# Band projections written out in eight trips, with turned rows copied straight to place and the norms regrouped

## Chip, cores and metric

One Trainium2 chip, one core. The metric is the device time of one launch in microseconds. Engines are named as the profile does: PE is TensorE, DVE VectorE, ACT ScalarE, POOL GpSimd, SP the queue that issues most DMAs.

## What is computed

The reference runs six residual blocks over x of shape (4, 1024, 128), float32. The fifth is a band attention; its beginning is what the changed function computes:

```python
invariant = _linear(x, Wproj, bproj)
residual = x - invariant
gauge = jnp.mean(jnp.linalg.norm(residual, axis=-1) / (jnp.linalg.norm(x, axis=-1) + 1e-08))
x_qk = jnp.where(gauge > GAUGE_THRESH, invariant, x)
Q = _linear(x_qk, Wq, bq)...
K = _linear(x_qk, Wk, bk)...
V = _linear(x, Wv, bv)...
```

Here x is the layer norm (without gain and bias) of the running rows: (x - m) / sqrt(v + 1e-5). The mean over all 4096 tokens must be known before the first Q and K row.

## The kernel before

The 4096 tokens lie in SBUF as X, 32 tiles of 128 tokens by 128 features. A trip takes 4 tiles (GROUP), so there are 8 trips; a block of 512 columns is the transposed rows of one trip. The stage runs from 1556.1 to 1636.7 us. Each engine has its own program, and counting semaphores alone set the order between them.

Before the first trip the outcome of the block in front is added to X: two partial results per token, in four quarters of 8 tiles (`add_back`, line 165), all on DVE. Quarter q holds the tiles of trips 2q and 2q + 1.

Trip j on each engine:
- DVE: `statistics(j)` (bn_stats, bn_aggr per tile) gives mean and variance; POOL turns variance into 1/sqrt (L2146, L2148, a power); DVE `normalise(j)` (L2167) writes xn.
- PE `turn_x(j)` (L2090) transposes four tiles into the PSUM bank x_ps. ACT `copy_x` (L2124) copies them to one of two buffers xs; DVE copies that buffer on to A.xnT (L2177).
- PE makes the gauge product inv_ps (L2096), 128x512; ACT adds the bias and stores it in A.invT (L2131); DVE forms res = x - invariant (L2182).
- ACT squares xs (L2129) and res (L2135); PE sums over features with a column of ones, eight matmuls of one column (L2108), each a weight load and a matmul in two passes, so 16 records a trip; DVE copies the eight columns from n_ps to A.norms (L2173).
- PE makes four value products v_ps (L2101); DVE adds the bias (L2186).

On PE the order in a trip is: gauge product of j, transposes of j+1, values of j, norms of j. The norms wait for both squares of j and, through `n_ready`, for DVE's copy of the norms of j-1, which stands behind the value copy of j on DVE. On ACT the order is: Square of xs (which waits for the norms of j-1), bias copy, copy_x of j+1, Square of res. Trips 1 to 4 are a hardware loop of two trips per pass, the others are written out. After the last trip ACT takes the square root of all norms, DVE adds 1e-8, inverts, multiplies and sums, PE adds up over partitions (L2116), and DVE compares with 0.3 into A.use_inv (L2222, L2224). The next stage, the queries (L2332 on), begins with that.

Of the kernel before, what the change touches and what calls it, by code (L numbers as in the profile page):

```python
# [12 lines left out]
ALU = mybir.AluOpType  # L13
# [3 lines left out]
P = 128  # L17
# [2024 lines left out]
def band_projections(nc, K, A, io, kept):  # L2042

    X, c = K.X, K.c
    with ExitStack() as ctx:
# [3 lines left out]
        stats, mv, var, rstd = sb("stats", [P, GROUP, 6]), sb("mv", [P, GROUP, 2]), sb("var", [P, GROUP]), sb("rstd", [P, GROUP])  # L2049
        xn, res = sb("xn", [P, GROUP, D]), sb("res", [P, BLOCK])  # L2050
        xs = [sb(f"xs{i}", [P, BLOCK]) for i in range(2)]
        squares = [sb(f"squares{m}", [P, BLOCK]) for m in range(2)]
        x_ps, inv_ps, v_ps, n_ps, w_ps, w_ps2 = (ps(n) for n in ("x_ps", "inv_ps", "v_ps", "n_ps", "w_ps", "w_ps2"))
        s = stage_sems(nc, ctx, "bp", "loaded passed turned kept ln_stats ln_mv ln_var ln_rstd xn_ready x_full xs_ready inv_full inv_ready "
                                     "v_full v_ready res_ready squares_ready n_full n_ready sqrt_ready gauge_step gauge_full joined")
        block = ctx.enter_context(nc.Block())
        SMALL = 10

        def in_projection_trips(eng, one_trip):

# [18 lines left out]
        @block.tensor  # L2079
        def _(pe):  # L2080
            for k in range(len(WEIGHTS)):
                bank = (w_ps, w_ps2)[k // 4]
                nc.tensor.transpose(bank[:, (k % 4) * P:(k % 4 + 1) * P], natural[:, k, :], c.ident[:, :])
            nc.tensor.transpose(w_ps2[:, P:P + 64], w1_natural[:, :], c.ident[0:64, 0:64]).then_inc(s.turned, 1)

            def turn_x(j):
                pe.wait_ge(s.xn_ready, j + 1)
                wait(pe, s.xs_ready, j)
                for t in range(GROUP):
                    last = nc.tensor.transpose(x_ps[:, t * P:(t + 1) * P], xn[:, t, :], c.ident[:, :])  # L2090
                last.then_inc(s.x_full, 1)

            def trip(j, p):
                pe.wait_ge(s.xs_ready, j + 1)
                wait(pe, s.inv_ready, j)
                nc.tensor.matmul(inv_ps[:, :], A.wT[:, 3, :], xs[p][:, :], start=True, stop=True).then_inc(s.inv_full, 1)  # L2096
                if not (isinstance(j, int) and j == TRIPS - 1):
                    turn_x(j + 1)
                wait(pe, s.v_ready, j)
                for t in range(GROUP):  # L2100
                    last = nc.tensor.matmul(v_ps[:, t * P:(t + 1) * P], xs[p][:, t * P:(t + 1) * P], A.wT[:, 2, :], start=(t == 0), stop=True,  # L2101
                                            skip_group_check=True)
                last.then_inc(s.v_full, 1)
                pe.wait_ge(s.squares_ready, at(j, 2, 2))
                wait(pe, s.n_ready, j)
                for t in range(GROUP):
                    for m in range(2):
                        last = nc.tensor.matmul(n_ps[:, 2 * t + m:2 * t + m + 1], squares[m][:, t * P:(t + 1) * P], A.ones[:, 0:1],  # L2108
                                                start=(t == 0 and m == 0), stop=True, skip_group_check=True)
                last.then_inc(s.n_full, 1)  # L2110

            turn_x(0)
            pe.wait_ge(s.kept, 3)
            in_projection_trips(pe, trip)
            pe.wait_ge(s.gauge_step, 5)
            nc.tensor.matmul(n_ps[:, 0:1], A.ones[:, :], A.norms[:, 0, 0:1], start=True, stop=True).then_inc(s.gauge_full, 1)  # L2116

        @block.scalar
        def _(act):
            def copy_x(j, p):  # L2120
                act.wait_ge(s.x_full, j + 1)
                wait(act, s.v_full, j - 1)
                wait(act, s.res_ready, j - 1)
                nc.scalar.copy(xs[p][:, :], x_ps[:, :]).then_inc(s.xs_ready, 1)  # L2124

            def trip(j, p):
                act.wait_ge(s.xs_ready, j + 1)
                wait(act, s.n_full, j)
                nc.scalar.activation(squares[1][:, :], xs[p][:, :], ACT.Square).then_inc(s.squares_ready, 1)  # L2129
                act.wait_ge(s.inv_full, j + 1)  # L2130
                nc.scalar.activation(A.invT[:, bass.ds(j * BLOCK, BLOCK)], inv_ps[:, :], ACT.Identity, bias=proj_bias).then_inc(s.inv_ready, 1)  # L2131
                if not (isinstance(j, int) and j == TRIPS - 1):
                    copy_x(j + 1, 1 - p)
                act.wait_ge(s.res_ready, j + 1)
                nc.scalar.activation(squares[0][:, :], res[:, :], ACT.Square).then_inc(s.squares_ready, 1)  # L2135

            copy_x(0, 0)
            in_projection_trips(act, trip)
            act.wait_ge(s.n_ready, TRIPS)
            nc.scalar.activation(A.norms[:, :, :], A.norms[:, :, :], ACT.Sqrt).then_inc(s.sqrt_ready, 1)  # L2140

        @block.gpsimd
        def _(pool):
            def trip(j, p):
                pool.wait_ge(s.ln_mv, j + 1)
                nc.gpsimd.tensor_tensor(var[:, :], mv[:, :, 1], c.eps[:, 0:GROUP], ALU.add).then_inc(s.ln_var, 1)  # L2146
                pool.wait_ge(s.ln_var, j + 1)
                nc.gpsimd.tensor_tensor(rstd[:, :], var[:, :], c.minus_half[:, 0:GROUP], ALU.pow).then_inc(s.ln_rstd, 1)  # L2148

            in_trips(pool, trip)  # L2150

        @block.vector
        def _(dve):
            def statistics(j):
                for t in range(GROUP):
                    last = nc.vector.bn_stats(stats[:, t, :], X[:, j * GROUP + t, :])
                last.then_inc(s.ln_stats, 1)
                wait_alone(dve, s.ln_stats, j + 1, s.passed)
                for t in range(GROUP):
                    last = nc.vector.bn_aggr(mv[:, t, :], stats[:, t, :])  # L2160
                last.then_inc(s.ln_mv, 1)

            def normalise(j):
                dve.wait_ge(s.ln_rstd, j + 1)
                wait(dve, s.x_full, j)
                for t in range(GROUP):
                    last = nc.vector.tensor_scalar(xn[:, t, :], X[:, j * GROUP + t, :], mv[:, t, 0:1], rstd[:, t:t + 1],  # L2167
                                                   ALU.subtract, ALU.mult)
                last.then_inc(s.xn_ready, 1)

            def keep_norms(j):
                dve.wait_ge(s.n_full, j + 1)
                nc.vector.tensor_copy(A.norms[:, bass.ds(j * GROUP, GROUP), :], n_ps[:, 0:2 * GROUP].rearrange("p (t m) -> p t m", m=2)).then_inc(s.n_ready, 1)  # L2173

            def trip(j, p):
                dve.wait_ge(s.xs_ready, j + 1)
                nc.vector.tensor_copy(A.xnT[:, bass.ds(j * BLOCK, BLOCK)], xs[p][:, :])  # L2177
                if not (isinstance(j, int) and j == TRIPS - 1):
                    normalise(j + 1)
                dve.wait_ge(s.inv_ready, j + 1)  # L2180
                wait(dve, s.squares_ready, at(j, 2, 0))
                nc.vector.tensor_tensor(res[:, :], xs[p][:, :], A.invT[:, bass.ds(j * BLOCK, BLOCK)], ALU.subtract).then_inc(s.res_ready, 1)  # L2182
                if not (isinstance(j, int) and j >= TRIPS - 2):
                    statistics(j + 2)
                dve.wait_ge(s.v_full, j + 1)
                nc.vector.tensor_tensor(A.v[:, bass.ds(j * GROUP + 1, GROUP), :], v_ps[:, :].rearrange("p (t d) -> p t d", d=P),  # L2186
                                        v_bias.unsqueeze(1).broadcast_to([P, GROUP, P]), ALU.add).then_inc(s.v_ready, 1)
                if not (isinstance(j, int) and j == 0):
                    keep_norms(j - 1)

            nc.vector.memset(A.ones[:, :], 1.0)
            nc.vector.memset(A.tiny[:, :], 1e-10)
# [5 lines left out]
            statistics(0)  # L2198
            normalise(0)
# [839 lines left out]
```

## Time and profile before

| | |
|---|---|
| median of 3 runs | 2554.82 us (2554.65 to 2556.2) |
| profiled execution, first to last instruction | 2555.3 us |
| mean granted TensorE clock | 0.838 |
| busy share PE / DVE / ACT / POOL | 78% / 77% / 55% / 41% |
| the stage | 80.6 us, 3.2% of the span |

The profile is one execution, recorded in hardware. Its span lies 0.5 us above the median of the runs. The shares are averages over stages with different limits and say little about this one; here the timeline of single engines counts.
### The profile page before, as it was taken

The numbers are of one execution on the slowest core, as the hardware profiler recorded it, in microseconds if no ns is written. First come the engines' busy times: TensorE is split into PE (matmuls) and PEld (weight loads), VectorE is DVE, ScalarE is ACT, GpSimd is POOL, SyncE is SP. The second block draws the span as 40 slices with busy tenths as digits, with TensorE's granted clock in tenths as the row PEclk, the third lists the DMA queues.
The fourth block names the chain that finished last, engine by engine and source line by source line (L and its number), as shares of the span: only waits on it lengthen the run. The fifth ranks groups of instructions, "written<-read, shape, count | busy, mean of one in ns | idle before, by whom it ended". The sixth has DMA issues, their size and how long they took to land. (4 is left out here: it accounts for less than half of the span.)

```text
span 2555.3 us, 85621 instructions
## 1 busy us (share of the span) xinstructions
PE 2005.7 (78%) x34294; PEld 1619.8 (63%) x34294; DVE 1955.3 (77%) x4641; ACT 1416.9 (55%) x2304; POOL 1039.6 (41%) x961
## 2 busy tenths in 40 slices
PE   3779399999999998669578994764666667769994
PEld 3668388888888887558457993552222234547894
DVE  5889589999999997779764444597999978855443
ACT  1647244444444443447455551367999978737452
POOL 3757355544444453666565662004000000036563
PEclk7889699999999998679879996685555578869997
DMA  5133200000000000022332222003333200031324
GB/s 124 47 98 111 86 3 0 0 0 0 0 0 0 0 0 3 31 82 88 117 105 81 70 69 81 0 0 52 63 50 63 35 2 1 2 90 46 92 77 122
DMA packets 103658, 120.90 MB, mean 47 GB/s; under 512 B 23224, under 2 KB 85288, under 8 KB 102848
## 3 DMA queue, kind: packets, MB, share of 16 engines
q1 hardware_dynamic: 82544, 80.39, 13.1%
q0 software_dynamic: 18176, 37.79, 4.4%
q8 instruction: 96, 1.57, 0.2%
q10 hardware_dynamic: 2768, 0.55, 0.2%
q14 instruction: 74, 0.61, 0.1%
HBM read 60.00 MB, written 46.20 MB: 42 GB/s over the span
## 5 line engine op out<-in xcount | busy, mean ns | idle before, releaser
L2521 DVE CUSTOM_DVE_ANT_0 be_logs<-be_joint,be_logs 128x1024 f32<-128x1024 f32 x256 | 293.3, 1222 | 10.2 <-ACT be_logs L2504 9.2
L2504 ACT ACTIVATE be_logs<-be_joint,b_tiny 128x1024 f32<-128x1024 f32 x256 | 283.7, 1114 | 19.7 <-PE be_joint L2489 11.8
L2489 PE MATMUL be_joint<-be_parts_k,be_parts_q 64*128 64x512 f32 x512 | 202.3, 789 | 108.9 <-DVE be_sums L2521 91.4
L446 POOL DMA_INDIRECT d_pairs<-s_y_tile,s_x_tiles x156 | 178.7, 1145 | 128.9 <-DVE s_y_tile L1404 104.4
L2489 PEld LDWEIGHTS be_joint<-be_parts_k,be_parts_q 64*128 64x128 f32 x512 | 73.7, 285 | 237.3 <-DVE be_sums L2521 216.5
L1764 POOL TENSOR_TENSOR m_roped_q<-m_raw_q,kg_xn 128x512 f32<-128x512 f32 x64 | 82.4, 1288 | 327.0 <-ACT m_raw_q L1686 327.0
L559 POOL IOTA s_xn<- 128x32 int32 x2 | 0.5, 253 | 487.1 <-POOLq L63 487.1
L446 POOL DMA_INDIRECT d_pairs<-g_y_tile,g_x_tiles x156 | 158.0, 1013 | 92.4 <-ACT g_y_tile L894 60.9
L1404 DVE TENSOR_SCALAR s_y_tile<-s_ps_y,s_x_tiles 128x128 f32<-128x128 f32 x156 | 47.5, 346 | 149.1 <-PE s_ps_y L1238 149.1
L1238 PE MATMUL s_ps_y<-s_down,s_a_tile 128*128 x1248 | 151.7, 275 | 0.0
L1238 PEld LDWEIGHTS s_ps_y<-s_down,s_a_tile 128*128 128x128 f32 x1248 | 145.9, 192 | 0.0
L1515 PE MATMUL m_front<-m_xnT,m_w_rot 128*128 128x128 f32 x1024 | 143.4, 284 | 3.2 <-DVE m_turned_q L1820 3.2
L1314 ACT ACTIVATE s_a_tile<-s_ps_h,s_tile_bias 128x256 f32<-128x256 f32 x312 | 122.5, 475 | 34.9 <-PE s_ps_h L1221 34.9
L1515 PE MATMUL m_front<-m_xnT,kg_xn 128*128 128x128 f32 x1024 | 138.9, 284 | 0.6 <-ACT m_xnT L1671 0.6
L1515 PEld LDWEIGHTS m_front<-m_xnT,m_w_rot 128*128 128x128 f32 x1024 | 126.0, 194 | 7.6 <-DVE m_turned_q L1820 3.4
L1515 PEld LDWEIGHTS m_front<-m_xnT,kg_xn 128*128 128x128 f32 x1024 | 124.1, 195 | 6.8 <-DVE m_w_rot L1955 0.9
L1724 ACT COPY m_oT<-m_back 128x1024 f32<-128x1024 f32 x32 | 32.5, 1017 | 127.1 <-PE m_back L1614 127.1
L1686 ACT COPY m_raw_q<-m_front 128x512 f32<-128x512 f32 x64 | 37.5, 585 | 111.1 <-PE m_front L1515 111.1
L776 PE MATMUL g_ps_h<-g_x_hi,g_up_tile 128*128 128x256 f32 x312 | 97.4, 312 | 1.5 <-DVE g_up_tile L1012 0.5
L1219 PE MATMUL s_ps_h<-s_x_hi,s_up_tile 128*128 128x256 f32 x312 | 96.0, 308 | 3.1 <-issue 3.1
L1909 DVE TENSOR_TENSOR m_mem<-m_mem,m_back 128x1040 f32<-128x1040 f32 x64 | 78.7, 1230 | 15.0 <-PE m_back L1598 14.6
L1220 PE MATMUL s_ps_h<-s_x_hi,s_up_tile 128*128 128x256 f32 x312 | 89.3, 286 | 0.0
(501 smaller groups left out, 6303.7 us busy)
## 6 DMA issues: line engine op xcount, KB each, us to landing
g_x_tiles<-d_rows SPq DMA_DIRECT2D x78, 132.0 KB, 2.1
s_x_tiles<-d_rows SPq DMA_DIRECT2D x78, 132.0 KB, 2.1
d_rows<-d_rows SPq DMA_DIRECT2D x32, 132.0 KB
s_down<-L_ffn_We SPq DMA_DIRECT2D x16, 256.0 KB, 6.0
be_parts_q<-be_high_q SPq DMA_DIRECT2D x64, 64.0 KB, 2.3
be_parts_q<-b_soft_q SPq DMA_DIRECT2D x64, 64.0 KB, 2.3
be_parts_k<-be_high_k SPq DMA_DIRECT2D x60, 64.0 KB, 2.3
be_parts_k<-b_soft_k SPq DMA_DIRECT2D x60, 64.0 KB, 2.3
```

The lines of the kernel that those rows point to most:

```text
L446: nc.gpsimd.indirect_dma_start(out=pairs[:, :], out_offset=bass.IndirectOffsetOnAxis(ap=x_tile[i % LOADS_AHEAD][:, h, D:D + 1].bitcast(U32 ...
L776: nc.tensor.matmul(h, up_tile[b][:, 0, m, part, :], x_hi[b][:, 0:SLOT_ROWS], start=(k % 2 == 0), stop=False, skip_group_check=True)
L1219: nc.tensor.matmul(h, up_tile[b][:, 0, chunk], x_hi[b][:, 0:SLOT_ROWS], start=(k % 2 == 0), stop=False, skip_group_check=True)
L1220: nc.tensor.matmul(h, up_tile[b][:, 1, chunk], x_hi[b][:, 0:SLOT_ROWS], start=False, stop=False, skip_group_check=True)
L1238: last = nc.tensor.matmul(y, a_tile[b][:, k, h * P:(h + 1) * P], down[:, bass.ds(experts[i], 1), k * D:(k + 1) * D], start=False, stop=(k ...
L1314: nc.scalar.activation(a_tile[b][:, k, :], ps_h[2 * b + k // 2][:, (k % 2) * SLOT_ROWS:(k % 2 + 1) * SLOT_ROWS], ACT.Silu, bias=tile_bias[ ...
L1515: last = nc.tensor.matmul(front_ps[bank][:, k * P:(k + 1) * P], weights[:, column + k * P:column + (k + 1) * P], xnT[:, :], start=(k == 0) ...
L1764: nc.gpsimd.tensor_tensor(roped[k][:, part, :], raw[k][:, part, :], wide(cos).broadcast_to([P, 4, P]), ALU.mult).then_inc(s.cos_done, 1)
L1909: nc.vector.tensor_tensor(part, part, back_ps[:, :, 0:4 * AUG].rearrange("p b (c e) -> p b c e", e=AUG), ALU.add).then_inc(s.mem_done, 1)
L2489: last = nc.tensor.matmul(joint_ps[k % DEPTH][:, a, :], parts[b % 2][0][rows, i * P:(i + 1) * P], parts[b % 2][1][rows, half * 512:(half + ...
L2504: nc.scalar.activation(logs[k % DEPTH][:, :, :], joint_ps[k % DEPTH][:, :, :], ACT.Ln, bias=A.tiny[:, :]).then_inc(s.log_ready, 1)
L2521: nc.vector.tensor_tensor_reduce(out=flat, in0=joint_ps[k % DEPTH][:, :, :].rearrange("p a j -> p (a j)"), in1=flat, scale=1.0, scalar=0.0 ...
```

## The change

1. The transposed rows are copied from PSUM straight into A.xnT, whose block j then serves as operand; the buffers xs and the copy L2177 go.
2. The residual norms of trip j are summed on PE behind the values of trip j+1, into columns of n_ps of their own for all 32 tiles; the copies to A.norms in each trip go, and the root reads PSUM.
3. The norm of x is taken from the layer norm: 128 times variance times 1/(v + 1e-5). The Square of x and half of the norm matmuls go; two small DVE operations come in trip 6.
4. The statistics have room for all 32 tiles, and all eight trips are written out on every engine.
5. The additions of quarters 2 and 3 move from DVE to POOL (`add_late`), four of 128x1024. DVE does statistics(1) ahead of normalise(0).
6. A first root on one column stands at the start of ACT's program; the x norms' root and reciprocal need not wait for the last residual norms.

```diff
+        xs = [A.xnT[:, j * BLOCK:(j + 1) * BLOCK] for j in range(TRIPS)]
+        inv = [A.invT[:, j * BLOCK:(j + 1) * BLOCK] for j in range(TRIPS)]
...
+            def residual_norms(j):
+                pe.wait_ge(s.squares_ready, j + 1)
                 for t in range(GROUP):
-                    for m in range(2):
-                        last = nc.tensor.matmul(n_ps[:, 2 * t + m:2 * t + m + 1], squares[m][:, t * P:(t + 1) * P], A.ones[:, 0:1],
+                    last = nc.tensor.matmul(n_ps[:, j * GROUP + t:j * GROUP + t + 1], squares[:, t * P:(t + 1) * P], A.ones[:, 0:1],
...
+            for j in range(TRIPS):
+                gauge_input(j)
+                if j + 1 < TRIPS:
+                    turn_x(j + 1)
+                values(j)
+                if j:
+                    residual_norms(j - 1)
+            residual_norms(TRIPS - 1)
...
+            act.wait_ge(s.warmed, 1)
+            nc.scalar.activation(warm[:, :], A.tiny[:, :], ACT.Sqrt)
+            copy_x(0)
+            for j in range(TRIPS):
+                act.wait_ge(s.inv_full, j + 1)
+                nc.scalar.activation(inv[j], inv_ps[:, :], ACT.Identity, bias=proj_bias).then_inc(s.inv_ready, 1)
+                if j + 1 < TRIPS:
+                    copy_x(j + 1)
+                act.wait_ge(s.res_ready, j + 1)
                 wait(act, s.n_full, j)
+                nc.scalar.activation(squares[:, :], res[:, :], ACT.Square).then_inc(s.squares_ready, 1)
+            act.wait_ge(s.norm_step, 2)
+            nc.scalar.activation(A.norms[:, :, 1], x_norm[:, :], ACT.Sqrt).then_inc(s.sqrt_ready, 1)
+            act.wait_ge(s.n_full, TRIPS)
+            nc.scalar.activation(A.norms[:, :, 0], n_ps[:, 0:TILES], ACT.Sqrt).then_inc(s.sqrt_ready, 1)
...
+            def add_late(q):
+                pool.wait_ge(kept.back_in[q], 32)
+                for m in range(2):
+                    if m:
+                        pool.wait_ge(s.joined_late, 2 * (q - 2) + 1)
+                    nc.gpsimd.tensor_tensor(X[:, quarter(q), :], X[:, quarter(q), :], kept.back[m][:, quarter(q), :], ALU.add).then_inc(s.joined_late, 1)
+
+            inverse_deviations(0)
+            inverse_deviations(1)
+            add_late(2)
+            inverse_deviations(2)
+            add_late(3)
+            for j in range(3, TRIPS):
+                inverse_deviations(j)
...
-            for q in range(1, 4):
-                add_back(nc, dve, X, kept.back, q, kept.back_in[q], s.joined)
-            dve.wait_ge(s.joined, 8)
-            statistics(1)
-            in_projection_trips(dve, trip)
-            keep_norms(TRIPS - 1)
+            add_back(nc, dve, X, kept.back, 1, kept.back_in[1], s.joined)
+            dve.wait_ge(s.joined, 4)
+            for j in range(TRIPS):
+                if j + 1 < TRIPS:
+                    normalise(j + 1)
+                residual(j)
+                if j + 2 < TRIPS:
+                    statistics(j + 2)
...
+                keep_values(j)
```

On TensorE before, trips 1 and 2 in the loop body (bp_inv_ps is the gauge product, bp_x_ps the transposes, bp_v_ps the values, bp_n_ps the norms):

```order
L2096 MATMUL bp_inv_ps<-bp_xs,b_wT 128x512
L2087 REGISTER_ALU
L2090 MATMUL bp_x_ps<-ident,bp_xn 128x128 x4
L2101 MATMUL bp_v_ps<-b_wT,bp_xs 128x128 x4
L2104 ISA
L2108 MATMUL bp_n_ps<-b_ones,bp_squares 128x1 x8
L2096 MATMUL bp_inv_ps<-bp_xs,b_wT 128x512
```

And in the changed kernel, trips 0 and 1:

```order
L2091 MATMUL bp_inv_ps<-b_xnT,b_wT 128x512
L2085 MATMUL bp_x_ps<-ident,bp_xn 128x128 x4
L2096 MATMUL bp_v_ps<-b_wT,b_xnT 128x128 x4
L2091 MATMUL bp_inv_ps<-b_xnT,b_wT 128x512
L2085 MATMUL bp_x_ps<-ident,bp_xn 128x128 x4
L2096 MATMUL bp_v_ps<-b_wT,b_xnT 128x128 x4
L2103 MATMUL bp_n_ps<-b_ones,bp_squares 128x1 x4
```

The norms have moved behind the values of the next trip, and there are four matmuls of them, not eight.

On GpSimd, the start of its program in the stage, as a difference (bp_rstd is 1/sqrt of a trip; ks_wide and ks_xn are the two partial results added to X):

```order
 L2146 TENSOR_TENSOR bp_var<-bp_mv,eps 128x4
 L2148 TENSOR_TENSOR bp_rstd<-bp_var,minus_half 128x4
-L2145 REGISTER_ALU
+L2155 TENSOR_TENSOR X<-X,ks_wide 128x1024
+L2155 TENSOR_TENSOR X<-X,ks_xn 128x1024
 L2146 TENSOR_TENSOR bp_var<-bp_mv,eps 128x4
 L2148 TENSOR_TENSOR bp_rstd<-bp_var,minus_half 128x4
-L73 REGISTER_ALU
-L73 COMPARE_AND_BRANCH
+L2155 TENSOR_TENSOR X<-X,ks_wide 128x1024
+L2155 TENSOR_TENSOR X<-X,ks_xn 128x1024
```

Two additions stand between the second and the third 1/sqrt, two more between the third and the fourth.

## Rows read from the trace of the kernel before

**Rows 1.** Busy time by stretch: the trips 1 to 7, then the query stage.

```profile
core 0: us, PE busy (x) PEld busy (x) DVE busy (x) ACT busy (x) POOL busy (x), PEclk, DMA share, GB/s
...
1580.10:1633.10 53.00, 43.09 (x207) 35.02 (x206) 23.43 (x90) 18.31 (x28) 6.03 (x10) 0.71 0.00 0
...
1636.70:1722.00 85.30, 55.81 (x221) 43.37 (x222) 78.89 (x100) 48.95 (x61) 0.00 (x0) 0.80 0.00 0
```

**Rows 2.** Timeline of PE: start, duration, line, tiles, idle before and releaser.

```profile
1576.37 1.92 PE L2101 MATMUL bp_v_ps<-b_wT,bp_xs 128*128 128x128 f32 x8
...
1580.04 1.10 PE L2096 MATMUL bp_inv_ps<-bp_xs,b_wT 128*128 128x512 f32 x2
1580.98 0.60 PE L2090 MATMUL bp_x_ps<-ident,bp_xn 128*128 128x128 f32 x4
1581.42 1.06 PE L2101 MATMUL bp_v_ps<-b_wT,bp_xs 128*128 128x128 f32 x8
1584.99 3.14 PE L2108 MATMUL bp_n_ps<-b_ones,bp_squares 128*128 128x1 f32 x16 [2.52 <-DVE b_norms L2173]
1587.99 2.05 PE L2096 MATMUL bp_inv_ps<-bp_xs,b_wT 128*128 128x512 f32 x2
...
1616.40 3.55 PE L2108 MATMUL bp_n_ps<-b_ones,bp_squares 128*128 128x1 f32 x16 [1.01 <-DVE b_norms L2173]
1619.81 2.05 PE L2096 MATMUL bp_inv_ps<-bp_xs,b_wT 128*128 128x512 f32 x2
...
1626.65 2.06 PE L2096 MATMUL bp_inv_ps<-bp_xs,b_wT 128*128 128x512 f32 x2
...
1631.13 1.92 PE L2108 MATMUL bp_n_ps<-b_ones,bp_squares 128*128 128x1 f32 x16 [0.95 <-DVE b_norms L2173]
```

**Rows 3.** Waits in the stage: who for whom, us in total, times, longest.

```profile
PE bp_n_ps L2108 <- DVE b_norms L2173: 9.9, 7, 2.5
```

**Rows 4.** Timeline of ACT in trip 2.

```profile
1590.18 0.69 ACT L2131 ACTIVATE b_invT<-bp_inv_ps,ks_xn 128x512 f32 x1 [1.32 <-PE bp_inv_ps L2096]
1590.94 0.58 ACT L2124 COPY bp_xs<-bp_x_ps 128x512 f32<-128x512 f32 x1
1591.81 0.63 ACT L2135 ACTIVATE bp_squares<-bp_res 128x512 f32<-128x512 f32 x1 [0.29 <-DVE bp_res L2182]
```

**Rows 5.** Timeline of DVE: an addition and normalise(1) at the start, then trip 3.

```profile
1564.10 1.22 DVE L165 TENSOR_TENSOR X<-X,ks_wide 128x1024 f32<-128x1024 f32 x1
...
1574.29 1.11 DVE L2167 TENSOR_SCALAR bp_xn<-X,bp_mv,bp_rstd 128x128 f32<-128x128 f32 x4 [1.18 <-POOL bp_rstd L2148]
...
1598.75 0.69 DVE L2182 TENSOR_TENSOR bp_res<-bp_xs,b_invT 128x512 f32<-128x512 f32 x1 [3.02 <-ACT b_invT L2131]
1599.36 0.87 DVE L2156 BATCH_NORM_STATS2 bp_stats<-X 128x6 f32 x4
...
1602.15 1.11 DVE L2167 TENSOR_SCALAR bp_xn<-X,bp_mv,bp_rstd 128x128 f32 x4 [0.42 <-POOL bp_rstd L2148]
```

**Rows 6.** Groups of POOL by form: busy, mean ns of one, idle before.

```profile
L1769 POOL TENSOR_TENSOR m_roped_q<-m_roped_q,m_turned_q 128x1024 f32<-128x1024 f32 x32 | 75.8, 2369 | 0.0
...
L2148 POOL TENSOR_TENSOR bp_rstd<-bp_var,minus_half 128x4 f32<-128x4 f32 x8 | 8.1, 1011 | 0.6
```

**Rows 7.** Timeline of POOL and DVE in the memory stage, where both work.

```profile
287.40 1.62 POOL L1764 TENSOR_TENSOR m_roped_q<-m_raw_q,kg_xn 128x512 f32<-128x512 f32 x1 [1.02 <-ACT m_raw_q L1686]
...
287.97 1.07 DVE L1963 TENSOR_SCALAR m_one_less_beta<-m_beta 128x16 f32<-128x16 f32 x1
...
305.86 3.46 POOL L1769 TENSOR_TENSOR m_roped_k<-m_roped_k,m_turned_k 128x512 f32<-128x512 f32 x2 [4.22 <-DVE m_turned_k L1820]
...
308.13 2.28 DVE L165 TENSOR_TENSOR X<-X,kg_wide 128x1024 f32<-128x1024 f32 x1
```

**Rows 8.** Timeline of DVE behind the last norms.

```profile
1633.09 0.17 DVE L2173 COPY b_norms<-bp_n_ps 128x8 f32<-128x8 f32 x1 [2.10 <-PE bp_n_ps L2108]
...
1634.62 0.15 DVE L2220 COPY b_norms<-b_gate 128x1 f32<-128x1 f32 x1
...
1635.65 0.15 DVE L2224 TENSOR_SCALAR b_use_inv<-b_use_inv 128x1 f32<-128x1 f32 x1
```

More of the change, by code:

```diff
@@ L2091, in turn_x, with gauge_input, values @@
                 last.then_inc(s.x_full, 1)
-            def trip(j, p):
+            def gauge_input(j):
                 pe.wait_ge(s.xs_ready, j + 1)
                 wait(pe, s.inv_ready, j)
-                nc.tensor.matmul(inv_ps[:, :], A.wT[:, 3, :], xs[p][:, :], start=True, stop=True).then_inc(s.inv_full, 1)
-                if not (isinstance(j, int) and j == TRIPS - 1):
-                    turn_x(j + 1)
+                nc.tensor.matmul(inv_ps[:, :], A.wT[:, 3, :], xs[j], start=True, stop=True).then_inc(s.inv_full, 1)
+            def values(j):
                 wait(pe, s.v_ready, j)
                 for t in range(GROUP):
-                    last = nc.tensor.matmul(v_ps[:, t * P:(t + 1) * P], xs[p][:, t * P:(t + 1) * P], A.wT[:, 2, :], start=(t == 0), stop=True,
+                    last = nc.tensor.matmul(v_ps[:, t * P:(t + 1) * P], xs[j][:, t * P:(t + 1) * P], A.wT[:, 2, :], start=(t == 0), stop=True,
                                             skip_group_check=True)
                 last.then_inc(s.v_full, 1)
-                pe.wait_ge(s.squares_ready, at(j, 2, 2))
-                wait(pe, s.n_ready, j)
+            def residual_norms(j):
+                pe.wait_ge(s.squares_ready, j + 1)
                 for t in range(GROUP):
-                    for m in range(2):
-                        last = nc.tensor.matmul(n_ps[:, 2 * t + m:2 * t + m + 1], squares[m][:, t * P:(t + 1) * P], A.ones[:, 0:1],
-                                                start=(t == 0 and m == 0), stop=True, skip_group_check=True)
+                    last = nc.tensor.matmul(n_ps[:, j * GROUP + t:j * GROUP + t + 1], squares[:, t * P:(t + 1) * P], A.ones[:, 0:1],
+                                            start=(j == 0 and t == 0), stop=True, skip_group_check=True)
                 last.then_inc(s.n_full, 1)
@@ L2118, in _, with copy_x @@
+            pe.wait_ge(s.gauge_step, 4)
+            nc.tensor.matmul(n_ps[:, 2 * TILES:2 * TILES + 1], A.ones[:, :], A.gate[:, :], start=True, stop=True, skip_group_check=True).then_inc(s.gauge_full, 1)
         @block.scalar
         def _(act):
-            def copy_x(j, p):
+            def copy_x(j):
                 act.wait_ge(s.x_full, j + 1)
-                wait(act, s.v_full, j - 1)
-                wait(act, s.res_ready, j - 1)
-                nc.scalar.copy(xs[p][:, :], x_ps[:, :]).then_inc(s.xs_ready, 1)
@@ L2126, in trip @@
-            def trip(j, p):
-                act.wait_ge(s.xs_ready, j + 1)
-                wait(act, s.n_full, j)
[L2129 to L2140, printed above, removed]
+                nc.scalar.copy(xs[j], x_ps[:, :]).then_inc(s.xs_ready, 1)
+            act.wait_ge(s.warmed, 1)
[7 more added lines that the diff above has]
+                act.wait_ge(s.res_ready, j + 1)
+                wait(act, s.n_full, j)
+                nc.scalar.activation(squares[:, :], res[:, :], ACT.Square).then_inc(s.squares_ready, 1)
@@ L2154, in statistics @@
             def statistics(j):
-                for t in range(GROUP):
-                    last = nc.vector.bn_stats(stats[:, t, :], X[:, j * GROUP + t, :])
+                if j in (4, 6):
+                    dve.wait_ge(s.joined_late, j - 2)
+                for t in range(j * GROUP, (j + 1) * GROUP):
+                    last = nc.vector.bn_stats(stats[:, t, :], X[:, t, :])
                 last.then_inc(s.ln_stats, 1)
                 wait_alone(dve, s.ln_stats, j + 1, s.passed)
-                for t in range(GROUP):
+                for t in range(j * GROUP, (j + 1) * GROUP):
                     last = nc.vector.bn_aggr(mv[:, t, :], stats[:, t, :])
@@ L2166, in normalise @@
                 for t in range(GROUP):
[L2167 to L2168 removed]
+                    w = j * GROUP + t
+                    last = nc.vector.tensor_scalar(xn[:, t, :], X[:, w, :], mv[:, w, 0:1], rstd[:, w:w + 1], ALU.subtract, ALU.mult)
                 last.then_inc(s.xn_ready, 1)
[L2171 to L2173 removed]
@@ L2175, in trip, with keep_values @@
[L2175 to L2179, printed above, removed]
-                dve.wait_ge(s.inv_ready, j + 1)
[L2181 to L2189, printed above, removed]
+            def keep_values(j):
+                dve.wait_ge(s.v_full, j + 1)
+                nc.vector.tensor_tensor(A.v[:, j * GROUP + 1:(j + 1) * GROUP + 1, :], v_ps[:, :].rearrange("p (t d) -> p t d", d=P),
+                                        v_bias.unsqueeze(1).broadcast_to([P, GROUP, P]), ALU.add).then_inc(s.v_ready, 1)
@@ L2191, in _, with residual @@
+            def residual(j):
+                dve.wait_ge(s.inv_ready, j + 1)
+                wait(dve, s.squares_ready, j)
+                nc.vector.tensor_tensor(res[:, :], xs[j], inv[j], ALU.subtract).then_inc(s.res_ready, 1)
+            nc.vector.memset(A.tiny[:, :], 1e-10).then_inc(s.warmed, 1)
             nc.vector.memset(A.ones[:, :], 1.0)
-            nc.vector.memset(A.tiny[:, :], 1e-10)
             for padded in (A.v, A.knT):
@@ L2198, in _ @@
             statistics(0)
+            statistics(1)
             normalise(0)
```

40 lines of the change are left out of this document (18 added, 22 removed).

## The prediction

> **What bounds the stage now.** I read the engines' totals by stretch first, because the change lies in one stage of some 80 us out of 2555.3: 1556.1 to 1636.7 us. From the first full trip to the last norm the stretch takes 53.0 us; TensorE is busy 43.1 of it, VectorE 23.4, ScalarE 18.3, at a mean granted clock of 0.71 [rows 1]. I call the start of trip j's gauge product on TensorE T(j). The timeline of TensorE gives T(1) = 1580.04, T(2) = 1587.99, T(6) = 1619.81, T(7) = 1626.65 [rows 2], so a trip lasts 8.0 us on the mean and the last full one 6.8. The reader is to see the gap before the norm products: in trip 1 TensorE waits 2.52 us there, and the grouped waits put 9.9 us in seven such gaps on the copy of the last trip's norms [rows 2, 3]. Behind the norm products stand the next gauge product and, on ScalarE, the squares of x and the copy of the next rows. So one trip is one ring: gauge product, ScalarE's bias copy, VectorE's residual, statistics, value copy and norm copy, sixteen norm records, next gauge product. TensorE cannot be kept full because the norms of trip j stand ahead of the gauge product of trip j+1.
>
> **Prices of TensorE's parts.** The two clock levels both stand in the rows (1.2 GHz is granted 0.5, 2.4 GHz is 1.0). The length of an operation, measured to the next start, is about 0.2 us less than the duration shown. At the low level: gauge product 1.85 (2.05 shown), value products 1.7 (1.92 shown), norms 3.41 (1616.40 to 1619.81). At the high level: 0.94, transposes 0.44, values 0.86, norms 1.77 (1.92 shown, less 0.15) [rows 2]. Transposes at the low level are twice 0.44, about 0.88.
>
> **Part by part.**
> Norms of x from the statistics: eight of the sixteen norm records of a trip go, so 1.7 us at the low clock and 0.88 at the high one; a Square of 0.63 us leaves ScalarE, which is not full. Norms a trip later: the wait of 9.9 us in all goes. Rows copied to place: 0.42 us of VectorE a trip, and the norm copy of 0.15 goes too; VectorE has the room already.
>
> *The new ring.* TensorE's own work in a trip is at the low clock 1.85 + 0.88 + 1.7 + 1.7 = 6.1 us, at the high clock 0.94 + 0.44 + 0.86 + 0.88 = 3.1. What is late next is the statistics chain, which spans two trips: gauge product (1.1 high, 2.05 low), ScalarE's bias copy with handoff 0.83, residual with handoff 0.74 [rows 4, 5], from the statistics' start to the start of normalise 2.79 (1599.36 to 1602.15, with GpSimd's power between), normalise 1.15, then transposes, values, norms 2.2 (high) up to T(j+2). That is 8.8 us per two trips, 4.4 a trip, at the high clock; at the low one 2.05 + 0.83 + 0.74 + 2.79 + 1.15 + 4.3 = 11.9, 5.9 a trip, so there TensorE's 6.1 binds. VectorE needs 1.1 + 0.6 + 1.3 + 0.6 = 3.6 a trip and does not bind. Which level? Full stretches of the old loop had 0.71 with TensorE busy 81%; the query stage after it has 0.80 with TensorE busy only 65% [rows 1]. The new ring at the high level is busy 3.1 of 4.4, 71%, with gaps of about 1.3 us instead of 2.5. I take about 0.85, that is 70% of the time high, and 4.9 us a trip. Bounds: 4.4 and 6.1.
>
> *The start, where I expect a cost.* Until T(0) nothing changes; statistics(1) goes into a wait of VectorE for GpSimd. Then VectorE adds back only quarter 1 instead of quarters 1 to 3: four additions of 1.22 us and 0.03 between, about 5 us, leave it, and normalise(1), at 1574.29 before [rows 5], could start at 1566.6. But the four additions run on GpSimd now, where a 128x1024 addition took 2.37 us [rows 6]; the first starts at about 1563.6, 1.5 us after statistics(1), by when GpSimd has its second power of 1.01 us [rows 6] behind it. The trace of the memory stage shows what happens when both engines read SBUF: GpSimd's product ran 287.40 to 289.02, and a VectorE tensor_scalar of only 128x16 begun at 287.97 took 1.07 us, to the same end; VectorE's addition of this very line, 1.22 us alone, took 2.28 us beside GpSimd's pair at 305.86 to 309.32 [rows 7]. They take turns. So I let them alternate: GpSimd 63.6 to 65.95, VectorE's first addition to 67.05, GpSimd's second to 69.3, VectorE's second to 70.4 (instead of 66.5). Normalise(1) to 71.5, residual(0) to 72.1, statistics(2) to 73.5, GpSimd's power to 74.8. There GpSimd goes on with the third addition, to 77.3, ahead of normalise(2), which VectorE reaches at 75.1 (values of trip 0 done) and which reads X: one of its four parts gets in at 77.3, the rest behind the fourth addition, 80.6. Transposes 0.9, values 1.7, norms of trip 0 1.7 at the low clock: T(2) = 1584.9. Against 1587.99 that is 3.1 us. If the two engines did not meet at all, the same chain gives T(2) = 1576.5. These are the ends; if every part of normalise(2) waited and handoffs grew, 1586.
> The Trainium skill (SBUF — State Buffer, "SBUF: two separate sides") holds that GpSimd and VectorE share a port pair as an exclusive lock for the whole instruction, and counts both a two-input VectorE operation and a two-port mode of tensor_scalar among the losers. That rule speaks against moving additions to GpSimd, and the memory stage agrees (1.07 us for 128x16). By it the start costs the 8.4 us between the two T(2); without it nothing.
>
> *Trips 2 to 6.* T(2) to T(7) took 1626.65 - 1587.99 = 38.7 us; now 5 x 4.9 = 24.5. Gain 14.2 (bounds 8.2 and 16.7).
>
> *The last trip.* From T(7) to the last norm record it was 6.4 us (1631.13 + 1.92 - 1626.65) [rows 2]. Now values, norms of trip 6 and, behind the last Square, norms of trip 7: 4.5 at the high clock, 6.9 at the low one; I take 5.3. Gain 1.1.
>
> *The tail.* From the last norm record at 1633.05 to the end of the second use_inv at 1635.80 it was 2.75 us [rows 8]. The copy out of PSUM (0.17 and 0.04), the addition (0.18), the reciprocal (0.35 + 0.04) and the copy of the sum (0.15) leave the path, since the x norms are ready early; root, product, sum, matmul, compare stay: 0.29 + 0.23 + 0.22 + 0.64 + 0.39 = 1.77. Gain 1.0. The table load of the root moves to the stage's start, where ScalarE is idle until 1564.5; it was hidden before too: nothing. The two small VectorE operations of x_norm in trip 6 lie in VectorE's gap before the values: nothing, 0.4 us without that cover.
>
> Sum: 3.1 + 14.2 + 1.1 + 1.0 = 19.4 us of the profiled 2555.3 us. The median of the runs, 2554.82, lies 0.5 below that span; I take the gain off the median: 2535.4 us.
>
> **Rivals.**
> *The additions don't collide.* For it: GpSimd's short power operations never lengthened a VectorE copy in this stage. Against it: rows 7. T(2) = 1576.5, 8.4 us more gain: 2527.
> *TensorE stays at the low level.* For it: the trips at 0.5 in the old loop followed directly on stretches in which TensorE had been held up, and trip 2 begins so. Against: 65% busy sufficed for 0.80 in the next stage. 5 x 6.1 = 30.5, last trip 6.9: 7.6 us less gain: 2543.
> *Written-out code gains by itself.* The old trips show no price of the loop: T(1) to T(2), inside the body, took 7.95; the four trips T(2) to T(6), two of them over the branch back, averaged 7.96 [rows 2]. So it gives nothing in my sum. If branches had held up engines other than TensorE, 4.4 a trip would be reached: 2532. The Trainium skill (Runtime: NRT & Kernel Launch, "Instruction fetch mechanics") says that a taken branch breaks sequential prefetch and calls this one reason for unrolling; by that rule the written-out form is the faster, which the two averages do not bear out.
> *The ring only moves its wait.* If residual, squares and bias copy on ScalarE in their new order hold each other up, trips stay above 7 us: 5 x 7.4 = 37, gain 1.7 instead of 14.2, and with the waits at the start not above 3: about 2551. Against it: ScalarE has 1.9 us of work a trip.
> *Slower: the query stage.* It lasts 85.3 us, VectorE is busy 78.9 of it and TensorE 55.8 at 0.80 [rows 1]. If its clock stayed at 0.5 after the changed entry, TensorE's work would be 55.8 x 0.8 / 0.5 = 89 us, more than the stage, and with the waits of one for the other about 110: 25 us more, 6 more than the change gives: 2560. It decides from a mean clock in that stage below about 0.55. Against it: nothing in that stage is touched, and it starts at 0.5 now.
>
> **Chances.** Forecast 0.58 (own range 2531 to 2540), no collision 0.16, low clock 0.16, code gain 0.04, wait moved 0.04, slower 0.02. 0.2%, 5.1 us, is about what this measurement can tell from no change. Faster 0.94, same 0.04, slower 0.02. The range 2525 to 2543.5 leaves out the last two and the ends of the second and third.
>
> **What would show it.** Right: GpSimd rows of 128x1024 at about 1563.6 and 1575, VectorE's quarter-1 additions with about 1.9 and 3.3 us, T(2) near 1585, then trips of 4.4 to 6 us with no wait before the norm products, transposes waiting on normalise instead; a tail of 1.8 us. Wrong: additions of 1.22 us beside GpSimd's; a clock of 0.5 from T(2) to T(7); trips above 7; or a query stage that differs from 85.3 us by more than 2.

## The result, and the profile after

| | before | changed |
|---|---|---|
| median | 2554.74 us (2554.15 to 2556.2, 4 runs) | 2530.57 us (2527.92 to 2534.04, 4 runs) |
| ratio, 95% interval | | 0.9905 [0.989, 0.992] |
| span of the profiled execution | 2555.3 us | 2526.1 us |
| the stage, first weight transpose to first query operation | 80.5 us | 57.7 us |

The change gains 24.2 us by the medians; forecast were 19.4, to 2535.4 us. The stage itself gains 22.9 us in the profiled executions. The spans differ by 29.2 us, and the other 6.3 lie in stages whose code is the same: the stage begins 2.1 us earlier, from its end to the first entropy product it is 113.1 instead of 114.4 us, and from the last entropy product to the end 508.5 instead of 511.3. These pieces wander: the kernel of experiment 4, whose last stages are those of before, had 507.1 where before had 511.3. So I judge by the stage from here on.

With j's start T(j) counted from the first weight transpose, the four terms of the sum came out so:

| | before | forecast | changed |
|---|---|---|---|
| to T(2) | 31.8 us | 28.8 | 27.2 |
| T(2) to T(7) | 38.7 | 24.5 | 23.3 |
| T(7) to the last norm record | 6.4 | 5.3 | 4.6 |
| tail to the second use_inv | 2.75 | 1.77 | 1.58 |

Busy time by stretch in the changed kernel, trips 1 to 7 and the query stage (answering to rows 1; the columns are the same):

```profile
1571.80:1609.23 37.43, 28.41 (x159) 22.39 (x158) 26.61 (x83) 12.63 (x21) 11.29 (x13) 0.84 0.00 1
1611.71:1697.00 85.29, 58.01 (x227) 45.80 (x228) 78.88 (x100) 49.06 (x61) 0.00 (x0) 0.78 0.00 0
```

TensorE's busy time fell from 43.1 to 28.4 us, and the stretch by 15.6 us: its waits are hardly shorter in sum, 9.0 against 9.9 us. The granted clock is 0.84 instead of 0.71 [rows 1]. The second stretch is cut to the length of that of before, so its length says nothing; its clock is 0.78 instead of 0.80, and the query stage up to the first entropy product took 113.1 instead of 114.4 us.

Timeline of PE, trips 2 to 6 of the changed kernel (answering to rows 2):

```profile
1581.28 1.10 PE L2091 MATMUL bp_inv_ps<-b_xnT,b_wT 128*128 128x512 f32 x2
...
1584.62 1.10 PE L2091 MATMUL bp_inv_ps<-b_xnT,b_wT 128*128 128x512 f32 x2
1587.71 1.11 PE L2085 MATMUL bp_x_ps<-ident,bp_xn 128*128 128x128 f32 x4 [2.00 <-DVE bp_xn L2183]
1588.62 1.91 PE L2096 MATMUL bp_v_ps<-b_wT,b_xnT 128*128 128x128 f32 x8
1590.33 1.17 PE L2103 MATMUL bp_n_ps<-b_ones,bp_squares 128*128 128x1 f32 x8
1591.36 1.10 PE L2091 MATMUL bp_inv_ps<-b_xnT,b_wT 128*128 128x512 f32 x2
...
1594.54 1.10 PE L2091 MATMUL bp_inv_ps<-b_xnT,b_wT 128*128 128x512 f32 x2
1597.79 1.12 PE L2085 MATMUL bp_x_ps<-ident,bp_xn 128*128 128x128 f32 x4 [2.15 <-DVE bp_xn L2183]
```

There is no wait before the norms of trips 0 to 6 any more; only the last group waits, 0.78 us for its Square. The wait stands before the transposes, on normalise, in every second trip: trips 2 to 6 last 3.34, 6.74, 3.18, 6.98 and 3.10 us. The short ones were granted 1.00, the long ones 0.75 and 0.76. Two trips together are 10.1 us, the two-trip chain of statistics at a mixed clock (8.8 and 11.9 were its ends). In the grouped waits of the stage, five waits for normalise, those of the start among them, stand where rows 3 had seven for the copy of the norms:

```profile
PE bp_x_ps L2085 <- DVE bp_xn L2183: 17.8, 5, 5.6
...
PE bp_n_ps L2103 <- ACT bp_squares L2136: 0.8, 1, 0.8
```

The start, first DVE and then POOL (answering to rows 5 to 7):

```profile
1562.02 2.67 DVE L165 TENSOR_TENSOR X<-X,ks_wide 128x1024 f32<-128x1024 f32 x1
1564.72 3.25 DVE L165 TENSOR_TENSOR X<-X,ks_xn 128x1024 f32<-128x1024 f32 x1
1568.01 1.12 DVE L2183 TENSOR_SCALAR bp_xn<-X,bp_mv,bp_rstd 128x128 f32<-128x128 f32 x4
...
1572.65 5.07 DVE L2183 TENSOR_SCALAR bp_xn<-X,bp_mv,bp_rstd 128x128 f32<-128x128 f32 x4
```

```profile
1561.26 2.35 POOL L2155 TENSOR_TENSOR X<-X,ks_wide 128x1024 f32<-128x1024 f32 x1
1563.69 3.20 POOL L2155 TENSOR_TENSOR X<-X,ks_xn 128x1024 f32<-128x1024 f32 x1
...
1572.38 2.34 POOL L2155 TENSOR_TENSOR X<-X,ks_wide 128x1024 f32<-128x1024 f32 x1
1574.80 2.34 POOL L2155 TENSOR_TENSOR X<-X,ks_xn 128x1024 f32<-128x1024 f32 x1
```

The turns can be read off the ends of the rows. GpSimd's first addition ends at 1563.61, VectorE's, begun at 1562.02, at 1564.69: 1.08 us after it. GpSimd's second begins at 1563.69, waits for that and ends at 1566.89; VectorE's second ends 1.08 us after that again. Normalise(2), four small operations of 0.34 us each, takes 5.07 us until both of GpSimd's other additions are through. Its first operation ends between the two additions, and the second lasts 2.49 us.

The tail on DVE (answering to rows 8):

```profile
1608.29 0.18 DVE L2226 TENSOR_SCALAR b_norms<-b_norms 128x32 f32<-128x32 f32 x1 [0.51 <-ACT b_norms L2138]
...
1609.58 0.19 DVE L2231 TENSOR_TENSOR b_curv<-b_curv,b_norms 128x32 f32<-128x32 f32 x1 [0.72 <-ACT b_norms L2140]
...
1610.66 0.15 DVE L2237 TENSOR_SCALAR b_use_inv<-b_use_inv 128x1 f32<-128x1 f32 x1
```

The addition and the reciprocal for the x norms run while the last residual norms are still being made, and 1.58 us are left behind 1609.23, where these end.

### The profile page after: what moved, and what is told of

It is laid out like the page before. It is cut to its first block and busy times, and to the rows that moved or that the text cites. A ratio compares the mean times of both kernels' runs of the same rounds, so it can differ in the third digit from the quotient of the medians.

```text
span 2526.1 us, 85364 instructions
## 1 busy us (share of the span) xinstructions
PE 1983.1 (79%) x34230; PEld 1601.6 (63%) x34230; DVE 1953.4 (77%) x4622; ACT 1412.7 (56%) x2298; POOL 1056.9 (42%) x965
## 5 line engine op out<-in xcount | busy, mean ns | idle before, releaser
L1724 ACT COPY m_oT<-m_back 128x1024 f32<-128x1024 f32 x32 | 32.6, 1018 | 127.0 <-PE m_back L1614 127.0
L1219 PE MATMUL s_ps_h<-s_x_hi,s_up_tile 128*128 128x256 f32 x312 | 95.9, 308 | 3.2 <-issue 1.6
L1769 POOL TENSOR_TENSOR m_roped_k<-m_roped_k,m_turned_k 128x512 f32<-128x512 f32 x64 | 88.3, 1392 | 6.2 <-DVE m_turned_k L1820 5.2
```

The costliest lines, as they stand in the source:

```text
L1219: nc.tensor.matmul(h, up_tile[b][:, 0, chunk], x_hi[b][:, 0:SLOT_ROWS], start=(k % 2 == 0), stop=False, skip_group_check=True)
L1769: nc.gpsimd.tensor_tensor(roped[k][:, part, :], roped[k][:, part, :], turned[k][:, part, :], ALU.add).then_inc(s.rope_done, 1)
```

## The experiments

Stage times are from one profile each. The time ratios are to the kernel before, on the same chip. All runs are in this table; the last two ran on a chip on which the kernel before took 2648.7 us. The experiments ran on three chips and there is one profile of the kernel before, so stage times of different chips stand side by side. The changed kernel's stage, profiled on two chips, was 57.7 and 58.2 us.

| | stage us | to T(2) | T(2) to T(7) | clock there | ratio, 95% interval |
|---|---|---|---|---|---|
| before | 80.5 | 31.8 | 38.7 | 0.68 | |
| changed | 57.7 | 27.2 | 23.3 | 0.85 | 0.9905 [0.989, 0.992] |
| 1 additions on DVE, in pairs | 57.9 | 18.6 | 32.2 | 0.73 | 0.9922 [0.9903, 0.9941] |
| 2 no late additions | 50.4 | 18.6 | 24.7 | 0.86 | 0.9868 [0.9852, 0.9885] |
| 3 norms in the same trip | 58.8 | 27.9 | 23.9 | 0.90 | 0.9917 [0.9901, 0.9934] |
| 4 before, written out | 83.7 | 32.6 | 40.6 | 0.62 | 0.9997 [0.9981, 1.0012] |
| 5 x squares back | 66.7 | 29.6 | 25.8 | 0.87 | 0.9929 [0.9909, 0.995] |
| 6 statistics ahead | 56.3 | 27.7 | 21.2 | 0.88 | 0.9881 [0.9851, 0.9911] |
| 7 statistics ahead, pairs on DVE | 54.8 | 18.0 | 29.7 | 0.77 | 0.988 [0.9849, 0.9911] |
| 8 before, own columns | 68.0 | 31.4 | 27.7 | 0.82 | 0.9939 [0.9919, 0.9959] |
| 9 one addition a trip | 50.5 | 18.9 | 24.3 | 0.86 | 0.9887 [0.9859, 0.9916] |
| 10 changed, again | 58.2 | 27.9 | 22.8 | 0.93 | 0.9925 [0.9899, 0.9951] |

**1. The additions on VectorE.**

```diff
-            add_late(2)
-            add_late(3)
...
                 if j in (4, 6):
-                    dve.wait_ge(s.joined_late, j - 2)
+                    add_back(nc, dve, X, kept.back, j // 2, kept.back_in[j // 2], s.joined)
+                    dve.wait_ge(s.joined, j + 2)
```

> Changed kernel, but the additions of quarters 2 and 3 stay on VectorE, each ahead of the statistics that need it (trips 2 and 4). Theory (exclusive turns of GpSimd and VectorE at SBUF): VectorE's quarter-1 additions fall from 2.67 and 3.25 us to 1.2 each, normalise(2) from 5.07 to 1.1 us, T(2) comes 6 to 7 us earlier; the two pairs of additions (2.5 us each) then lie in the statistics chain of trips 2 and 4 and cost 2 to 5 us; the stage lasts 53 to 56 us instead of 57.7. Rival (GpSimd's help is worth its price, VectorE binds): stage 58 to 62 us.

DVE in that kernel:

```profile
1565.04 1.21 DVE L165 TENSOR_TENSOR X<-X,ks_wide 128x1024 f32<-128x1024 f32 x1
1566.29 1.23 DVE L165 TENSOR_TENSOR X<-X,ks_xn 128x1024 f32<-128x1024 f32 x1
...
1572.34 1.12 DVE L2182 TENSOR_SCALAR bp_xn<-X,bp_mv,bp_rstd 128x128 f32<-128x128 f32 x4
...
1578.77 1.22 DVE L165 TENSOR_TENSOR X<-X,ks_wide 128x1024 f32<-128x1024 f32 x1
1580.03 1.23 DVE L165 TENSOR_TENSOR X<-X,ks_xn 128x1024 f32<-128x1024 f32 x1
...
1584.08 1.11 DVE L2182 TENSOR_SCALAR bp_xn<-X,bp_mv,bp_rstd 128x128 f32<-128x128 f32 x4 [0.82 <-POOL bp_rstd L2148]
```

The collision is shown: without GpSimd's additions VectorE's take 1.2 us, normalise(2) 1.12 instead of 5.07, and T(2) comes 8.6 us earlier (expected were 6 to 7; the forecast's ends lay 8.4 apart). But the expected stage of 53 to 56 us missed: T(2) to T(7) takes 8.9 us more, not 2 to 5. Trips 3 and 5, each behind a pair, last 8.9 and 8.7 us; TensorE waits 3.6 and 3.9 us in them, and the clock from T(2) to T(7) is 0.73. The pair stands between X and the statistics of a later trip and lengthens the chain itself. As ordered, GpSimd's help was worth what it cost, 57.7 against 57.9 us.

**2. Without those additions** (both `add_late` calls and the waits for them left out; that part of the sum is missing).

> Changed kernel without the additions of quarters 2 and 3 (that part of the computation is left out). It prices them by themselves. Theory: GpSimd's additions cost only through the turns, 3.9 us in the quarter-1 additions and 3.9 in normalise(2), less a wait of TensorE: stage 57.7 - 7 = about 51 us. Rival (additions beside each other cost no more than VectorE's own work): stage within 1 us of 57.7.

50.4 us, as expected: the four additions cost the changed kernel 7.3 us. T(2) comes 8.6 us earlier without them, and 1.3 of that are lost again from T(2) to T(7).

**3. Norms in the same trip.**

```diff
                 values(j)
-                if j:
-                    residual_norms(j - 1)
-            residual_norms(TRIPS - 1)
+                residual_norms(j)
```

> Changed kernel with the residual norms of trip j again behind the values of trip j. Theory (the statistics chain over two trips binds now, not the norms): the short trips grow from 3.2 to about 4.3 us and the long ones shrink by as much, stage within 1.5 us of 57.7. Rival (the norms a trip later are the main gain): each trip from T(2) on gains the wait of square and residual, 1 us or more, stage 62 us or longer.

1.2 us longer, within the 1.5 expected and no more than one profile can tell. Norms wait again (2.5 us in five trips), but in time in which the next normalise is not done anyway. No worth of the norms a trip later by themselves is shown here.

**4. Before, written out** (`for j in range(TRIPS): one_trip(j, j % 2)` in place of the loop, on all engines).

> Kernel before with all eight trips of the stage written out and nothing else changed. Theory (the loop costs nothing): stage within 1 us of 80.6, time within 2 us of the kernel before. Rival (taken branches break prefetch, computed addresses cost): stage 3 us or more shorter.

The time ratio is 0.9997, so writing out gives nothing that the interval of 5 us less to 3 us more can tell. The stage was 3.2 us longer, against the expectation of 1 us, in the same order of work: some trips had norms of 3.5 us at 0.5 where before had 1.9 at 1.0, though the waits before the norms were shorter, 8.1 against 9.9 us. A stage's length is known to some 3 us only, as its clock falls.

**5. The x squares back.** The Square stands behind that of the residual, its four sums in front of the residual's.

```diff
+                nc.scalar.activation(squares_x[:, :], xs[j], ACT.Square).then_inc(s.squares_x_ready, 1)
...
+                pe.wait_ge(s.squares_x_ready, j + 1)
+                for t in range(GROUP):
+                    nc.tensor.matmul(n_ps[:, TILES + j * GROUP + t:TILES + j * GROUP + t + 1], squares_x[:, t * P:(t + 1) * P], A.ones[:, 0:1],
```

> Changed kernel with the Square of x on ScalarE and its four sums a trip on TensorE done again, beside the norm from the statistics (their result is not used). Theory (TensorE's norm records lie on the two-trip chain: transposes, values, norms): 0.9 us a record group at the high clock, 1.7 at the low one, in every second trip, and twice at the end: stage 4 to 8 us longer than 57.7. Rival (norms are hidden in TensorE's waits): under 2 us.

9.0 us longer, just above the 4 to 8 expected: 2.4 before T(2), 2.4 up to T(7), and 4.0 in the last trip, which has 8.6 us: both groups of records and the second Square stand at its end one behind the other. So the half of the norm work that the change saves would not have been hidden.

**6. Statistics ahead.**

```diff
-                residual(j)
                 if j + 2 < TRIPS:
                     statistics(j + 2)
-                else:
+                residual(j)
+                if j + 2 >= TRIPS:
```

> Changed kernel with statistics(j+2) ahead of residual(j) on VectorE, nothing else. Theory (from T(2) on the chain bias copy, residual, statistics, power, normalise binds): without its first links the long trips of 6.7 to 7.0 us shrink; all trips 3.4 to 4.0 us, T(2) to T(7) 17 to 20 us instead of 23.3, stage 52 to 55 us. Rival (VectorE's amount of work or TensorE's clock binds): within 1.5 us of 57.7.

DVE and then POOL in that kernel, trips 4 and 5:

```profile
1594.39 0.66 DVE L2194 TENSOR_TENSOR bp_res<-b_xnT,b_invT 128x512 f32<-128x512 f32 x1
...
1596.23 1.11 DVE L2183 TENSOR_SCALAR bp_xn<-X,bp_mv,bp_rstd 128x128 f32<-128x128 f32 x4 [0.58 <-POOL bp_rstd L2148]
```

```profile
1594.55 0.55 POOL L2146 TENSOR_TENSOR bp_var<-bp_mv,eps 128x4 f32<-128x4 f32 x1 [2.53 <-DVE bp_mv L2175]
```

After a trip of 5.51 us at 0.55 and one of 3.11 at 1.00, three trips last 4.18, 4.18 and 4.17 us at 1.00, and T(2) to T(7) is 21.2 us. The expectation missed: it had trips of 3.4 to 4.0 us, T(2) to T(7) in 17 to 20 and a stage of 52 to 55, and 56.3 lies where the rival had it, 1.4 us below the changed kernel, which one profile does not tell from no change. Even trips alone prove nothing either, as the changed kernel has them in experiment 10. What differs is their length at the same clock, 4.18 against 4.42 us, and the gap before the transposes, 0.87 against 1.11.

The rows show what binds now: normalise waits 0.58 us for the power of its own statistics, and from normalise to normalise VectorE and GpSimd take 4.17 us without TensorE. Part of it is a new collision: GpSimd's short addition in front of the power (L2146) stands beside the residual and takes 0.55 us instead of 0.20. Without that the round would be 3.8 us by this estimate, inside the expected range; no run tests it.

**7. Both** (the edits of experiments 1 and 6).

> Statistics ahead and the additions of quarters 2 and 3 on VectorE together. Theory: the start is 8 us shorter as with the additions on VectorE alone; with the statistics ahead each pair of additions delays the ring by its own 2.5 us at most and not by a chain of 3.9 and a slower clock: stage 48 to 51 us, faster than both kernels. Rival (VectorE is then full): 53 us or more.

54.8 us, above the expected 48 to 51 and in the rival's range: trips 3 and 5, each the one behind a pair, last 8.0 and 8.7 us. The pair still stood ahead of the statistics in the same trip.

**8. Before, written out, with columns of their own.**

```diff
-                wait(pe, s.n_ready, j)
...
-                        last = nc.tensor.matmul(n_ps[:, 2 * t + m:2 * t + m + 1], squares[m][:, t * P:(t + 1) * P], A.ones[:, 0:1],
-                                                start=(t == 0 and m == 0), stop=True, skip_group_check=True)
+                        last = nc.tensor.matmul(n_ps[:, at_column:at_column + 1], squares[m][:, t * P:(t + 1) * P], A.ones[:, 0:1],
+                                                start=(j == 0 and t == 0 and m == 0), stop=True, skip_group_check=True)
```

Here `at_column` is `2 * (j * GROUP + t) + m`; the copies by `keep_norms` go.

> Kernel before, written out, with columns of their own for all 32 tiles' norms in PSUM, so that TensorE no longer waits for VectorE's copy of the last norms; 16 norm records a trip and all else as before. Theory (that wait, 9.9 us in seven trips, was the largest single loss): stage 74 to 78 us where the written-out kernel had 83.7. Rival (the squares come no sooner, the wait only changes its name): 82 us or more.

PE in that kernel, trips 2 and 5:

```profile
1592.38 1.10 PE L2092 MATMUL bp_inv_ps<-bp_xs,b_wT 128*128 128x512 f32 x2
...
1595.65 1.95 PE L2104 MATMUL bp_n_ps<-b_ones,bp_squares 128*128 128x1 f32 x16 [0.56 <-ACT bp_squares L2131]
...
1612.55 1.95 PE L2104 MATMUL bp_n_ps<-b_ones,bp_squares 128*128 128x1 f32 x16 [0.84 <-ACT bp_squares L2131]
```

68.0 us, 15.7 less than the written-out kernel and 12.6 less than before, with nothing else of the order changed: more than the 74 to 78 us expected. The waits before the norms had been 9.9 us in before and 8.1 in experiment 4; 2.7 are left, for squares. So the waits alone do not make the gain. From T(2) to T(7) TensorE's idle time falls from 6.4 us (6.2 in experiment 4) to 1.7, and its busy time, with the same records, from 32.3 (34.4) to 26.0. The larger part of the gain there, 6.3 to 8.4 us against 4.5 to 4.7, is the clock, 0.82 instead of 0.68 and 0.62. In experiment 8 the norms from trip 1 on take 1.93 to 2.17 us, in 4 up to 3.54.

**9. One addition a trip.** As 7, but without `add_back` in `statistics`; instead:

```diff
                 residual(j)
+                if j < 4:
+                    add_one(2 + j // 2, j % 2)
```

where `add_one(q, m)` is one of the two additions of quarter q.

> Statistics ahead, and the four additions of quarters 2 and 3 on VectorE one by one, behind the residuals of trips 0 to 3, where VectorE waits for the values or for GpSimd's power. Theory: no addition lies between X and the statistics of the next trips any more; each adds 0.6 us to a trip of 4.2 to 4.5 and no jump to 8 us as with pairs; T(2) at 18.5 to 19.5, T(2) to T(7) 21 to 24, stage 50 to 52 us. Rival (VectorE's 3.6 us a trip and the 1.2 fill it, pairs or singles are alike): 54 us or more.

DVE, POOL and PE in that kernel, around trip 2:

```profile
1649.73 1.22 DVE L2199 TENSOR_TENSOR X<-X,ks_xn 128x1024 f32<-128x1024 f32 x1
...
1651.85 1.11 DVE L2181 TENSOR_SCALAR bp_xn<-X,bp_mv,bp_rstd 128x128 f32<-128x128 f32 x4 [0.30 <-POOL bp_rstd L2148]
```

```profile
1649.95 1.86 POOL L2148 TENSOR_TENSOR bp_rstd<-bp_var,minus_half 128x4 f32<-128x4 f32 x1
```

```profile
1649.84 1.10 PE L2091 MATMUL bp_inv_ps<-b_xnT,b_wT 128*128 128x512 f32 x2
1653.02 0.66 PE L2085 MATMUL bp_x_ps<-ident,bp_xn 128*128 128x128 f32 x4 [2.08 <-DVE bp_xn L2181]
...
1655.22 1.11 PE L2091 MATMUL bp_inv_ps<-b_xnT,b_wT 128*128 128x512 f32 x2
```

50.5 us as expected. The four trips with an addition last 5.0, 4.8, 5.4 and, at a clock of 0.75, 6.6 us. All additions are done and the stage is as short as without them (50.4). Beside the changed kernel on the same chip it is 7.7 us shorter in the stage, and 2617.15 against 2627.54 us in the medians, though the ranges overlap (2605.98 to 2622.29, 2617.71 to 2635.05). Over experiments 6 and 7 the ratios show no lead: 0.9887 against 0.9881 and 0.988.

The additions are not hidden. Beside one, GpSimd's power takes 1.86 us instead of 1.01, and normalise waits for it. From normalise to normalise three of the four rounds with an addition take 5.03 us, the fourth 5.38. 5.03 is 0.86 more than the 4.17 of experiment 6, which is what the power loses, and more than the 0.6 expected.

**10. The changed kernel again.**

> The changed kernel once more, beside the kernel before on the same chip. Theory: the stage lasts 57.7 us again within 1 us (order and clock repeat), and the differences between runs of 5 us lie outside the stage. Rival: the stage itself varies by several us with the clock's phase.

58.2 us, within 1 us as expected, but order and clock did not repeat: even trips of 4.4 to 4.9 us at 0.93 this time, where the first profile had 3.1 and 7.0 in turns at 0.85. The last three last 4.42, 4.42 and 4.41 us at 1.00. Two such trips are 8.8 us, the chain at the high clock; that the alternation is only another phase of it is my reading and was not tested.

## Why the prediction was right

**The wait before the norms goes** held, and was the step worth most. But the prediction put the 9.9 us under "norms a trip later". Item 2 of the change has two parts, and that is the one that did not bring it: with the norms back in their own trip the stage is 1.2 us longer (experiment 3), while columns of their own, so that no copy stands in the ring, bring 12.6 to 15.7 us to the kernel before (experiment 8). From T(2) to T(7) that is 11.0 us of the 15.3 that the whole change gained there. Half the norm records come on top, 9.0 us in the stage if undone (experiment 5). These do not add up, since each was taken from another kernel.

**What is late next** held: statistics, power, normalise over two trips. In experiment 10 two trips at the high clock take 8.83 us for the 8.8 worked out, and with the first links taken away (experiment 6) a trip falls from 4.42 to 4.18 us. **4.9 us a trip at a clock of 0.85** came out as 4.67 at 0.85, and that is in part luck. The 0.85 was taken for a ring busy 71% of the time with gaps of 1.3 us. The measured one is busy 82% (19.2 of 23.3 us), has gaps of 2.0 to 2.2 us in every second trip, and its trips of 3.1 to 7.0 us lie outside the 4.4 to 6 named as a sign. The same kernel was granted 0.93 in experiment 10, with nearly the same time, 22.8 us.

**The start** held in mechanism and nearly in size. The quarter-1 additions ended at 1567.97, which on the clock of before is 1570.1 (70.4 forecast), and normalise(2) at 1577.72, or 1579.8 (80.6); that one of its four operations would get in between GpSimd's additions held too. The "1.9 us" named as a sign for VectorE's first addition does not fit the prediction's own chain, which gives 2.95 (64.1 to 67.05); 2.67 were measured. T(2) was 1.5 us earlier than forecast: 0.8 by the end of normalise(2) and 0.8 by norms of trip 0 that ran at a rising clock (0.88 us to the next start instead of 1.7), less 0.1 in the steps between. Experiment 1 gives 8.6 us between collision and none, where 8.4 were forecast.

**The last trip and the tail** gained 1.8 and 1.2 where 1.1 and 1.0 stood: the clock was 1.00 in the last trip, 4.61 us against 4.5 for that end, and the last partition sum took 0.38 instead of 0.58 us.

So all four terms were a little too small: 19.4 forecast, 22.9 measured in the stage. The median of 2530.57 us lies just below the forecast's own range of 2531 to 2540, and inside the outer one. The rivals: no collision is refuted by the rows and by experiment 1; the low clock by 0.85; a gain from writing out by experiment 4 (0.9997); a wait only moved by 23.3 us, though the wait before the transposes is real (its time of 2551 does not follow from its terms, which give about 2548); the query stage kept its 113 to 115 us to the first entropy product.

What stays open is why the pieces outside the stage differ by up to 4 us from run to run with unchanged code. It limits what the medians can say of the change, and it is why the stage is used here.

## What to carry to other kernels

Look for the small operation that stands in a ring only because a buffer is used again: eight PSUM columns copied out each trip held TensorE up, and a bank with room for all trips removed the copy and, with the clock that rose, gained more than the whole wait: 12.6 us where 9.9 had been waited, 15.7 where it was 8.1. Before work is moved to GpSimd, list which VectorE operations read SBUF in that time and which of GpSimd's, since here they took turns. Do not put a pair of additions between an input and the chain that binds: one piece a trip gave a stage of 50.5 us where pairs gave 54.8, by one profile each.

## What the hardware showed

GpSimd's 128x1024 addition stretched four VectorE operations of 0.34 us to 5.07 us, and VectorE's additions of 1.22 us to 2.67 and 3.25. GpSimd's own second addition became 3.20 instead of 2.35 us, so either side waits. VectorE's copies out of PSUM beside GpSimd's first addition, at 1561.69 and 1561.89, took 0.28 and 0.21 us as in the kernel before. GpSimd's short power operation did not do this: in the old kernel VectorE's copy of 128x512 at 1601.32 took 0.41 us inside the power of 1601.11 to 1602.12. But it gives way itself: 1.86 us instead of 1.01 beside VectorE's 128x1024 addition in experiment 9, and the short addition in front of it 0.55 instead of 0.20 beside the residual in experiment 6.

The clock amplified the largest change. From T(2) to T(7) the ring of before was granted 0.68 and 0.62 in two profiles of one order of work, and 0.82 with the waits before the norms cut from 9.9 and 8.1 us to 2.7.
